# Attention scores as pairs of 64-row array tiles, and maxima taken over two PSUM banks at once

## The reference, cut to what matters

```python
Q = split_heads(Xn @ Wq + bq); K = split_heads(Xn @ Wk + bk); V = split_heads(Xn @ Wv + bv)
scores = jnp.einsum('bhqd,bhkd->bhqk', Q, K) / jnp.sqrt(jnp.float32(D_HEAD))   # D_HEAD = 16
scores = jnp.where(causal, scores, jnp.float32(-jnp.inf))
A = jax.nn.softmax(scores, axis=-1)
AV = jnp.einsum('bhqk,bhkd->bhqd', A, V)
...
x = _layernorm(x + attention(x)); x = _layernorm(x + mixture(x))
```

## Time and profile before

| | |
|---|---|
| median of 3 runs | 511.62 us (510.28 to 512.27) |
| span of the profiled execution | 510.6 us |
| TensorE matmul busy | 454.6 us, 89% |
| TensorE weight loads (overlap the matmuls) | 265.5 us, 52% |
| VectorE busy | 324.8 us, 64% |
| ScalarE busy | 218.8 us, 43% |
| GpSimd busy | 71.0 us, 14% |

### The profile page before, as it was taken

The page is one execution under the profiler, slowest core; times in us unless marked ns, Lnnn a source line. Parts: engine busy times, 40 slices in busy tenths (PEclk is TensorE's granted clock), DMA queues, the critical chain, the costliest instruction groups (busy, mean ns, idle before and its releaser), DMA issues.

```text
span 510.6 us, 6947 instructions
## 1 busy us (share of the span) xinstructions
PE 454.6 (89%) x2512; PEld 265.5 (52%) x2512; DVE 324.8 (64%) x780; ACT 218.8 (43%) x470; POOL 71.0 (14%) x97
## 2 busy tenths in 40 slices
PE   0289799999999999999899995999999999999693
PEld 0145565556546554357557752555655554447352
DVE  6936588678778674526476894478868855114276
ACT  1132034666666756333421131466666757532110
POOL 9720010022011010100400010012102001010000
PEclk9999699999999999799999997699999999999897
DMA  5006990025002000000423195006100000000011
GB/s 165 0 10 108 213 161 7 3 46 83 3 0 85 2 2 1 0 1 3 117 66 62 36 168 89 1 3 112 15 1 2 3 2 1 0 1 1 0 42 42
DMA packets 13266, 21.18 MB, mean 41 GB/s; under 512 B 2352, under 2 KB 9776, under 8 KB 13232
## 3 DMA queue, kind: packets, MB, share of 16 engines
q1 hardware_dynamic: 13232, 20.73, 19.5%
HBM read 5.78 MB, written 2.10 MB: 15 GB/s over the span
## 4 chain that ended last, share of the span: by engine, by line
PE 77%; DVE 12%; ACT 4%; DMA 2%; issue 2%; SPq 2%; DVEq 0%; ACTq 0%
PE ps L691 24%; PE ps L758 18%; PE ps L778 15%; PE ps L736 13%; PE ps L740 3%; DVE mx L582 3%; DVE nv L521 2%; PE ps L685 2%; ACT pr L483 2%; SPq L388 1%; PE ps L788 1%; DVE st L533 1%; DMA stq<-mrow 1%; DVE x L540 1%; PE ps L823 1%
## 5 line engine op out<-in xcount | busy, mean ns | idle before, releaser
L483 ACT ACTIVATE pr<-ps 128x512 f32<-128x512 f32 (+3 forms) x384 | 171.7, 493 | 164.4 <-PE ps L758 162.6
L582 DVE TENSOR_REDUCE mx<-ps 128x1 f32<-128x512 f32 (+3 forms) x304 | 185.3, 655 | 58.9 <-PE ps L740 40.7
L758 PE MATMUL ps<-stq,stk 98*128 98x512 f32 (+3 forms) x384 | 146.0, 414 | 11.8 <-DMA stq<-mrow 6.7
L736 PE MATMUL ps<-stk,stq 96*128 96x512 f32 (+3 forms) x384 | 136.0, 391 | 3.6 <-DMA stq<-qk 1.4
L758 PEld LDWEIGHTS ps<-stq,stk 98*128 98x128 f32 x384 | 71.5, 197 | 83.2 <-ACT pr L483 44.5
L448 POOL TENSOR_SCALAR_AFFINE_SELECT pr<-pr 128x512 f32<-128x512 f32 x64 | 40.9, 639 | 359.1 <-ACT pr L483 359.1
L736 PEld LDWEIGHTS ps<-stk,stq 96*128 96x128 f32 x384 | 76.0, 200 | 14.5 <-DVE mx L582 5.5
L778 PE MATMUL ps<-pr,va 128*32 128x512 f32 (+3 forms) x768 | 83.5, 507 | 0.0
L740 PE MATMUL ps<-mask,ident_b 128*128 128x128 bf16 x256 | 58.8, 237 | 0.0
L740 PEld LDWEIGHTS ps<-mask,ident_b 128*128 128x128 bf16 x256 | 25.6, 100 | 30.9 <-issue 23.1
L691 PE MATMUL ps<-pr,w_qk 128*128 128x512 f32 x64 | 31.8, 646 | 3.8 <-ACT pr L462 3.8
(11 more groups left out here) (72 smaller groups left out, 340.1 us busy)
## 6 DMA issues: line engine op xcount, KB each, us to landing
stk<-qk SPq DMA_DIRECT2D x16, 256.0 KB, 3.8
stq<-qk SPq DMA_DIRECT2D x32, 128.0 KB, 3.8
x_in<-in_x SPq DMA_DIRECT2D x8, 256.0 KB, 3.5
stk<-qk SPq DMA_DIRECT2D x16, 128.0 KB, 3.7
stq<-qk SPq DMA_DIRECT2D x32, 64.0 KB, 3.1
out_y<-x SPq DMA_DIRECT2D x3, 512.0 KB, 2.9
qk<-in_x SPq DMA_DIRECT2D x2, 512.0 KB, 4.0
v_t<-in_vt SPq DMA_DIRECT2D x1, 512.0 KB, 5.8
```

What stands on the lines that cost most here:

```text
L483: nc.scalar.activation(probs(b, g, s)[:, j, q0 - c * CHUNK:], act_bank(ev)[:, q0 - c * CHUNK:], ACT.Exp, scale=DH ** -0.5).then_inc(s_act_ ...
L582: nc.vector.tensor_reduce(dst, src, AX.X, ALU.max).then_inc(s_dve_free, 1)
L736: last = nc.tensor.matmul(bank[:, i * w:(i + 1) * w], q[0:ROWS, t // TPC, j, tile(t % TPC)], k[0:ROWS, k0 // CHUNK, j % 2, 0:w], start=Tru ...
L758: nc.tensor.matmul(bank[:, q0 - c * CHUNK:], stk[stack_of(b, g)][0:ROWS + 2, kt // TPC, j % 2, tile(kt % TPC)], stq[stack_of(b, g)][0:ROWS ...
```

## The change

The zero rows go. Each head gets 48 rows plus its 2 rows of maxima in one half of the partitions: heads i = 0 and 1 of a pair stand at partitions 0 to 49 and 64 to 113 (`strip(i)`), and the two products of a pair are issued one after the other, on the two 64-row halves of the array, into two banks. `stq` shrinks from 4 copies to 2. A unit covers both heads of a pair, so it takes two adjacent banks, and one VectorE instruction reduces both: 20 units in a group instead of 38. The bank mask is added once per bank, for up to two heads in one instruction. A score pair takes two of ScalarE's three banks and waits for both. Each (group, chunk) stack is filled by 8 DMAs instead of 6, with the same 768 KB, and the maxima by 2 DMAs instead of 1. GpSimd fills `stk` with -1 and no longer clears `stq`. The order's numbers are halved where they count units (the opening has 9 units), and work beside a step stands after its first or its second pair.

```diff
-ROWS = 2 * 3 * DH
+ROWS = 3 * DH
+HALF = P // 2
...
-            n = 4 if w == P else 2 if w == 2 * P else 1
-            units += [(t, k0, w, tuple(range(j, j + n)), k0 + w == (t + 1) * P) for j in range(0, HPG, n)]
+            n = 2 if w <= 2 * P else 1
+            units += [(t, k0, w, m, n, k0 + w == (t + 1) * P) for m in range(0, 2, n)]
...
-    course = [(0, needed[0] + 6), (first_step[1], needed[1] + 8), (first_step[-1] - 3, needed[-1])]
+    course = [(0, needed[0] + 3), (first_step[1], needed[1] + 4), (first_step[-1] - 3, needed[-1])]
...
-        for j in range(HPG):
+        for m in range(2):
...
-                order.append(("score", b, *at[k], j))
-            issue_max(int(target(k + (j + 1) / HPG)))
+                order += [("score", b, *at[k], m, i) for i in range(2)]
+            issue_max(int(target(k + (m + 1) / 2)))
...
-        stq = [sb(f"stq{i}", [P, C, HPG, CHUNK], F32R) for i in range(STACKS)]
-        stk = [sb(f"stk{i}", [P, C, PAIRS, CHUNK], F32R) for i in range(STACKS)]
+        stq = [sb(f"stq{i}", [P, C, 2, CHUNK], F32R) for i in range(STACKS)]
+        stk = [sb(f"stk{i}", [P, C, 2, CHUNK], F32R) for i in range(STACKS)]
...
+        def dve_pair(ev):
+            return ps[:, dve_at[ev]:dve_at[ev] + 2, :]
+
+        def strip(i, n=ROWS):
+            return slice(i * HALF, i * HALF + n)
...
+                        both, one = strip(i, 2 * DH), slice(i * HALF + 2 * DH, i * HALF + ROWS)
                         high = qk[head, 0, 0, c].rearrange("p m s -> p (m s)").unsqueeze(1)
-                        loads += [(q[2 * i * DH:2 * (i + 1) * DH, c, 2 * i:2 * i + 2], high.to_broadcast([DH, 2, KC * CHUNK])),
-                                  (q[one.start + i * DH:one.start + (i + 1) * DH, c, 2 * i:2 * i + 2], qk[head, 0, 1, c])]
+                        loads += [(k[both, c], qk[head, 1, :, c]), (k[one, c], qk[head, 1, 0, c]),
+                                  (q[both, c], high.to_broadcast([DH, 2, KC * CHUNK])), (q[one, c], qk[head, 0, 1, c])]
...
-                    sp.dma_start(stq[stack_of(b, g)][ROWS:ROWS + 2, c].bitcast(F32),
-                                 mrow[:, c, :].bitcast(F32)).then_inc(s_rows[c], 16)
+                    for i in range(2):
+                        sp.dma_start(stq[stack_of(b, g)][i * HALF + ROWS:i * HALF + ROWS + 2, c].bitcast(F32),
+                                     mrow[i * 4 * TPC:(i + 1) * 4 * TPC, c, :].bitcast(F32)).then_inc(s_rows[c], 16)
...
-                    src = dve_bank(ev)[:, 0:len(heads) * w].rearrange("p (h k) -> p h k", k=w)
+                    src = dve_pair(ev)[:, :, 0:n * w].rearrange("p i (m k) -> p i m k", k=w)
                     nc.vector.tensor_reduce(dst, src, AX.X, ALU.max).then_inc(s_dve_free, 1)
...
-                    bank = take_dve(ev)
-                    for i, j in enumerate(heads):
-                        last = nc.tensor.matmul(bank[:, i * w:(i + 1) * w], q[0:ROWS, t // TPC, j, tile(t % TPC)],
-                                                k[0:ROWS, k0 // CHUNK, j % 2, 0:w], start=True, stop=not diagonal)
-                        if diagonal:
-
-                            last = nc.tensor.matmul(bank[:, (i + 1) * w - P:(i + 1) * w], ident_b[:], mask[:],
+                    take_dve(ev)
+                    banks = dve_pair(ev)
+                    for m in range(n):
+                        for i in range(2):
+                            last = nc.tensor.matmul(banks[:, i, m * w:(m + 1) * w], q[strip(i), t // TPC, m0 + m, tile(t % TPC)],
+                                                    k[strip(i), k0 // CHUNK, m0 + m, 0:w], start=(m == 0),
+                                                    stop=(m == n - 1 and not diagonal))
+                    if diagonal:
+
+                        for i in range(2):
+                            last = nc.tensor.matmul(banks[:, i, 0:n * w].rearrange("p (m k) -> p m k", k=w)[:, :, w - P:],
+                                                    ident_b[:], mask[:].unsqueeze(1).to_broadcast([P, n, P]),
                                                     start=False, stop=True)
...
-                    if kt == 0 and j == 0:
...
+                    if i == 0:
+
+                        if kt == 0 and m == 0:
...
+                            pe.wait_ge(s_rows[c], 32 * (b * G + g + 1))
+                        take_act(("score", b, g, s, m, 1))
                     bank = take_act(ev)
-                    nc.tensor.matmul(bank[:, q0 - c * CHUNK:], stk[stack_of(b, g)][0:ROWS + 2, kt // TPC, j % 2, tile(kt % TPC)],
-                                     stq[stack_of(b, g)][0:ROWS + 2, c, j, q0 - c * CHUNK:],
+                    nc.tensor.matmul(bank[:, q0 - c * CHUNK:],
+                                     stk[stack_of(b, g)][strip(i, ROWS + 2), kt // TPC, m, tile(kt % TPC)],
+                                     stq[stack_of(b, g)][strip(i, ROWS + 2), c, m, q0 - c * CHUNK:],
                                      start=True, stop=True).then_inc(s_act_full, 1)
```

78 lines of the change are left out of this document (39 added, 39 removed).

## The result

The changed kernel takes 544.25 us (median of 4 runs, 538.34 to 548.63), the kernel before beside it 510.95. The ratio is 1.062, with an interval of 1.055 to 1.068. The forecast was 511.3, with a range up to 528.

The account below looks back on a forecast made before the run. The prediction took TensorE to bound the kernel: -5.9 (attention) + 2.0 + 2.6 (SyncE's queue) + 1 + 0 = -0.3 on a 510.6 us span, 510.3, with the median 1.0 above: 511.3 us, range 498 to 528.

Parts of the forecast that it names:

- Terms (1) to (4): TensorE's pairs, late loads, masks, value steps and turns in 24 middle score steps: 56.6 us of work, 11.2 less than 67.8.
- no overlap: Rival: the two array halves do not overlap at all, +24 us, 535 us; chance 0.10.
- loads in series: Rival: the two weight loads of a pair run one after the other, +13 us, 524 us; chance 0.17.
- Changes of shape are free: Rival: switching between half and full array costs TensorE nothing, 8 us saved, 503 us; chance 0.23.
- Term (5): A step's second pair waits for ScalarE's banks, 1.25 us after the first at 512 columns: 9.0 us in 24 steps.
- Term (6): VectorE's maximum reductions, ring now two pairs deep: covered under TensorE's work, 0 us.
- Term (7): More DMA issues on SyncE's queue delay the openings: +2.0 us in b = 0, +2.6 in b = 1.
- Term (8): The rest: b = 1 opening units +1 us, last steps 0, GpSimd's smaller start-up fills 0.
- a rival with 0.08: TensorE's idle time drops the clock to half once in each of 8 groups: +28 us, 539 us; chance 0.08.
- the first two: Signs: a pair's products start within 0.02 us, the next about 0.23 later; a pair's two loads start nearly together.
- the third: Sign: a mask starts 0.3 us or more after its pair, 0.1 beyond the stream.
- the fourth: Sign: TensorE's largest idle is its wait for ScalarE, 1.25 us from first to second pair of a 512-wide step.

Follow-up runs that it names:

- all_remedies: Changed kernel with score and maximum pairs over all 128 rows, late start-up fills, 6 loads per stack part, Exp's scale 0.001: 517.05 us, ratio 1.011.
- fill_first_gap: Changed kernel with the gap behind each step's first score pair filled by repeated maximum pairs: 545.22 us, ratio 1.064.
- before_66_rows: Kernel before with score and maximum products on only the first 66 rows, Exp's scale 0.001: 531.77 us, ratio 1.040.
- all_64_rows: Changed kernel with score and maximum products over all 64 rows of each half, Exp's scale 0.001: 526.77 us, ratio 1.030.

## Why the prediction was wrong

- *Terms (1) to (4), TensorE's work.* Forecast 56.6 us of work in the 24 steps, measured 57.1 busy at the full clock (all_remedies, above). Pairs overlap, loads run side by side, and a change of shape costs 0.09 us where 0.10 was charged. The rivals "no overlap" and "loads in series" are out: the pair of 384 columns is followed after 0.28 us. "Changes of shape are free" is out by the 0.09.
- *Term (5), the bank wait.* Mechanism and floor right to 0.01 us (1.24 against 1.25). The size was a little too high: 6.6 us of idle time by ScalarE's banks in the 24 steps, 9.0 forecast. (By the prediction's own prices the waits at 384, 256 and 128 columns are 0.41, 0.30 and 0.15 us rather than 0.38, 0.24 and 0.1, which makes 9.6; the slip changes nothing.) The runs on the full array add that on the kernel before this wait costs 12 us, and the grouping of the scores by twos another 5, for which the sum had no term.
- *Term (6), VectorE's ring.* Set at 0 because a reduction of a pair takes 1.2 us and a unit comes every 1.2 to 1.9. It does take that (1222 ns for 1024 elements), but TensorE waited for it all the same, 1.6 + 1.5 + 0.2 = 3.3 us in 24 steps; by my reading units bunch up around masks and row maxima, and a ring of two pairs passes each bunch on. With this, 0.5 us for an `av_raw` wait and small gaps, TensorE's idle time is 68.35 - 57.10 = 11.25 us, and the steps took 68.35 us (all_remedies), where 65.6 were forecast and 67.2 measured before. The gain of 5.9 us was a loss: 1.1 x 181/67.2 = 3 us over the same stretches.
- *Term (7), SyncE's queue.* The issues of four stacks were set at 23 us, near the lower end of 21 to 28, reasoning that some are paced by their bytes. They came out at 26.5, close to the upper end: 32 issues at 0.83 us each on average, where 24 with the same bytes had taken 0.88. And the wait of b = 0 was sized from one part's two extra issues, while eight stand ahead of the second rows. Forecast 4.6 us, alone on the kernel before 16.
- *Term (8), the start.* GpSimd's fills were said to be covered by the wait for the first layer norm. They were its cause: 8.4 us sooner for TensorE's first product, 4.4 at the first value step.
- *The clock.* This is the step that failed: the sum leaves TensorE's granted clock as it was, and allows for its fall only in a rival with 0.08 that has idle time as the one trigger. Measured, the clock went from 0.961 to 0.856, with 147 us at half instead of 34, which is some 32 of the 33 us lost (an estimate, above). The rival's 539 us came near by luck: it had 56 us more at half (8 x 7), and 113 were measured, and its trigger is at best a part. Filling the gaps raised the clock by 0.03 and gave no time (fill_first_gap), taking rows away from the kernel without gaps cost 20 us (before_66_rows), and adding rows gave 17.5 us with the gaps in place (all_64_rows, with 4.9 us of later start already in it). A change from 98 rows to two halves of 50 wasn't looked at for what it does to the clock. Beside it, (5) and (6) together missed by 9 us, (7) by 11 as measured on the kernel before, and (8) by 4 the other way; a part of these runs through the clock too, so they can't simply be added.

Of the signs named ahead, the first two held; the third, the mask, came 0.27 us behind a 384-wide pair and 0.32 behind a 512-wide one; the fourth held for ScalarE's banks; the rows' DMA came 26.5 us behind the first stack DMA rather than 23. Neither of the two conditions for being wrong came: TensorE had idle time, and two 512-wide value steps of the middle stretch stood 3.06 us apart in the kernel after (91.83 to 94.89). It went wrong by the clock, for which no sign had been named.

## What to carry to other kernels

Before packing products into parts of the array, read the granted clock where the kernel now runs, and expect it to depend on the rows that the products use and not only on how busy TensorE is; a stage at the half clock took over 40% longer here (15.54 us for 10.84). Count DMAs of this size (64 to 256 KB), not bytes, at some 0.7 to 0.9 us each over all queues together, wherever a first product waits for the last of a row of them. And look at what GpSimd does while VectorE runs a tiny operation that takes microseconds: moving a few fills brought 10 us here, more than the 5.9 that the pairs were forecast to bring.

## What was not expected of the hardware

- Products over more rows, most of the added ones zeros, speed the kernel up. The mean clock went from 0.847 to 0.870 up to 0.906 to 0.919 when score pairs used 128 rows instead of 100 and maximum pairs 128 instead of 96, and from about 0.96 to 0.90 when the kernel before went from 98 and 96 rows to 66.
- At 66 rows TensorE stayed at the half clock for 41 us in which it was never idle.
- A TENSOR_SCALAR of 128x4 elements took 8.08 us beside GpSimd's fills, and 1.27 us without the large ones.
- A second queue brought little speed (0.70 us for each DMA instead of 0.78), and ScalarE did nothing else in that time.
